# Two key tiles weighed in one go, and whole-array jobs moved to the other gaps, in a 1444-key cross attention

## What is computed

```python
qm = _split_heads(q @ Wq.T + bq)
km = _split_heads(k @ Wk.T + bk)
vm = _split_heads(v @ Wv.T + bv)
scores = jnp.einsum('bnlh,bnph->bnlp', qm, km) / np.sqrt(HEAD_DIM)
scores = jnp.where(mask, scores, MASK_FILL)
attn = jax.nn.softmax(scores, axis=-1)
out = jnp.einsum('bnlp,bnph->bnlh', attn, vm)
out = out.transpose(0, 2, 1, 3).reshape(B, L, D_MODEL)
return out @ Wo.T + bo
```

## Time and profile before

| | |
|---|---|
| median of the runs | 2277.2 us |
| span of the profiled execution | 2267.4 us |
| stage B, from its first weighing to the end of the full clock | 602 to 1736 us |
| one group of four elements in stage B | 144.4 us, 36.1 per element |
| PE, DVE, ACT busy in stage B | 93%, 78%, 64% |
| granted TensorE clock in stage B | 1.00 |

### The profile page before, as it was taken

One profiled execution on the slowest core, in us unless ns is written; L12 is line 12 of the kernel. 1 busy time (PEld: TensorE's weight loads), 2 busy tenths in 40 slices (PEclk: granted clock), 3 DMA queues, 4 the chain that ended last, 5 costly groups with the idle time before them and its releaser, 6 DMA issues. The chain is left out here.

```text
span 2267.4 us, 43146 instructions
## 1 busy us (share of the span) xinstructions
PE 1969.0 (87%) x16922; PEld 1258.0 (55%) x16922; DVE 1578.2 (70%) x3726; ACT 1324.7 (58%) x2169; POOL 551.4 (24%) x477
## 2 busy tenths in 40 slices
PE   3679999667999999999999999999997888888997
PEld 2546666444556556565565655556564555555554
DVE  4845666795787877878788788878771566664554
ACT  3645776683366666666666666666664555553444
POOL 1411322314122212222221222222222132311122
PEclk9879999777799999999999999999998788788999
DMA  5025554012132323233131322313222001103441
GB/s 153 1 92 183 184 173 142 4 37 91 65 109 74 126 68 118 78 105 119 68 126 63 120 85 101 121 66 122 79 89 67 16 8 16 31 1 59 67 71 40
DMA packets 120023, 189.26 MB, mean 83 GB/s; under 512 B 36770, under 2 KB 94090, under 8 KB 118414
## 3 DMA queue, kind: packets, MB, share of 16 engines
q1 hardware_dynamic: 119822, 186.50, 26.6%
HBM read 103.33 MB, written 11.76 MB: 51 GB/s over the span
## 5 line engine op out<-in xcount | busy, mean ns | idle before, releaser
L1610 DVE TENSOR_REDUCE b_part_max<-psum 128x1 f32<-128x482 f32 (+3 forms) x1248 | 737.6, 651 | 188.1 <-PE psum L1487 174.1
L1400 ACT ACTIVATE b_PT<-psum 128x800 f32<-128x800 f32 x768 | 616.6, 836 | 386.1 <-PE psum L1506 381.1
L1487 PE MATMUL psum<-b_KH,b_QBD 64*128 64x482 f32 (+1 forms) x1152 | 422.6, 445 | 45.7 <-DVE b_part_max L1610 43.3
L1506 PE MATMUL psum<-b_QS,b_KS 64*128 64x200 f32 x3072 | 438.3, 288 | 0.5 <-ACT b_PT L1400 0.3
L1506 PEld LDWEIGHTS psum<-b_QS,b_KS 64*128 64x128 f32 x3072 | 339.4, 186 | 16.2 <-issue 11.8
L1522 PE MATMUL psum<-b_PT,b_V 128*32 128x200 f32 x6144 | 341.4, 339 | 0.6 <-ACT b_PT L1400 0.6
L1487 PEld LDWEIGHTS psum<-b_KH,b_QBD 64*128 64x128 f32 x1152 | 197.3, 189 | 198.6 <-DVE b_part_max L1610 118.4
L1322 POOL TENSOR_TENSOR b_KL<-b_KF,b_KH 128x1444 fp32r<-128x1444 f32 x32 | 106.8, 3338 | 693.3 <-PE psum L1506 670.1
L1522 PEld LDWEIGHTS psum<-b_PT,b_V 128*32 128x32 f32 x6144 | 159.9, 109 | 149.1 <-ACT b_PT L1400 82.3
L1900 ACT ACTIVATE c_HE<-psum,C 128x400 f32<-128x400 f32 x128 | 75.7, 595 | 94.6 <-PE psum L2116 90.1
L1474 PE MATMUL psum<-W,b_CT 128*128 128x128 f32 (+1 forms) x768 | 117.7, 293 | 12.6 <-DVE b_part_max L1610 6.7
(11 more groups left out here) (280 smaller groups left out, 3095.2 us busy)
## 6 DMA issues: line engine op xcount, KB each, us to landing
b_KS<-b_KH SPq DMA_DIRECT2D x64, 722.0 KB
a_CT<-in_ctxt SPq DMA_DIRECT2D x32, 722.0 KB, 5.5
b_CT<-in_ctxt SPq DMA_DIRECT2D x32, 722.0 KB, 4.4
b_KS<-b_KL SPq DMA_DIRECT2D x32, 722.0 KB
a_CN<-in_ctxn SPq DMA_DIRECT2D x32, 704.0 KB
att_scratch<-b_AO SPq DMA_DIRECT2D x32, 200.0 KB, 1.9
c_G<-gates_scratch SPq DMA_DIRECT2D x4, 1600.0 KB
c_KBD<-gates_scratch SPq DMA_DIRECT2D x4, 1600.0 KB
```

Source lines behind the costliest of these rows:

```text
L1400: nc.scalar.activation(PT[:, kt % 2, 2 * a:2 * a + 2, :], psum[:, 2 * a:2 * a + 2, 0:TG], ACT.Exp).then_inc(sem["pt_ready"], 1)
L1487: m = mm(bank(b, D, size), QBD[rows, j % 2, tile * D:(tile + 1) * D], KH[rows, j % 2, at_:at_ + size], start=True, stop=True)
L1506: m = mm(bank(p, D, 2 * T, (s % 2) * 2 * T), KS[rows, j % 2, s, kt * D:(kt + 1) * D], QS[rows, j % 2, s * 2 * T:(s + 1) * 2 * T], start=Tr ...
L1610: v.tensor_reduce(part_max[0:rows, q, c:c + 1], bank(b, rows, CHUNKS[c][1]), AX.X, ALU.max)\
```

## The change

Two key tiles are weighed one after the other after each odd slot, none after an even one. All whole-array jobs get the even slots: values 0, 2, 4 (before 2, 3, 4), left-over maxima 0, 4, 6 (before 5, 6, 7), keys 6, 8, 10 (before 6, 7, 8), the result 2 (before 1), the turn 8 as before, queries 0 and 10 (before 0 and 5). `PT` gets a third buffer. Four maximum jobs stand in slots 9, 10, 11, 0, 1 and 6, three in 2 to 5, none in 7 and 8; before it was four in 9, 10, 11 and 0, three in 1 to 6, two in 7, none in 8. In ACT's program a key chunk whose job is in slot s is now rounded after the exponentials of tile s + 1, as value chunks are copied.

```diff
-MAIN_TILES = ((9, 2, 2), (10, 2, 2), (11, 2, 2), (0, 2, 2), (1, 2, 1), (2, 1, 2), (3, 2, 1), (4, 1, 2), (5, 2, 1), (6, 1, 2), (7, 1, 1))
-QUERY_SLOTS = (((0, 0), (1, 0), (2, 0), (3, 5)), ((4, 0), (5, 5)), ((6, 0),), ())
+MAIN_TILES = ((9, 2, 2), (10, 2, 2), (11, 2, 2), (0, 2, 2), (1, 2, 2), (2, 1, 2), (3, 2, 1), (4, 1, 2), (5, 2, 1), (6, 2, 2))
+QUERY_SLOTS = (((0, 0), (1, 0), (2, 0), (3, 10)), ((4, 0), (5, 10)), ((6, 0),), ())
+VALUE_SLOTS, LEFT_SLOTS, KEY_SLOTS = (0, 2, 4), (0, 4, 6), (6, 8, 10)
+RESULT_SLOT, TURN_SLOT = 2, 8
...
-        PT = sb("PT", [D, 2, HG, TG])
+        PT = sb("PT", [D, 3, HG, TG])
...
                 if a == 0:
-                    wait(act, sem["pv_done"], n * KT + (kt - 1))
+                    wait(act, sem["pv_done"], n * KT + (kt - 2))
...
-                        if kt - 3 in range(len(highs)):
-                            value(*place(g, j, highs[kt - 3]), g, j + 1, kt - 3)
-                        if kt - 8 in range(len(keys)):
-                            high_keys(*place(g, j, keys[kt - 8]), g, j + 2, kt - 8)
+                        for i, at in enumerate(highs):
+                            if kt == VALUE_SLOTS[i] + 1:
+                                value(*place(g, j, at), g, j + 1, i)
+                        for i, at in enumerate(keys):
+                            if kt == KEY_SLOTS[i] + 1:
+                                high_keys(*place(g, j, at), g, j + 2, i)
...
                         some(PHASES * kt + 4)
-                        weigh(g, j, kt)
+                        if kt % 2:
+                            weigh(g, j, kt - 1)
+                            weigh(g, j, kt)
```

More of the change, by code:

```diff
@@ L1100, in ring_jobs @@
     after = not last or j + 2 < GROUP
-    jobs = [((g, j + 1, "result", 0), PHASES * 1 + 4)]
+    jobs = [((g, j + 1, "result", 0), PHASES * RESULT_SLOT + 4)]
     for i, (_, _, _, kt, p) in enumerate(MAINS):
@@ L1109, in ring_jobs @@
     if nxt:
-        jobs += [((g, j + 1, "value", r), PHASES * (r + 2) + 4) for r in range(3)]
-        jobs += [((g, j + 1, "max", len(MAINS) + c), PHASES * (c + 5) + 4) for c in range(3)]
-        jobs.append(((g, j + 1, "turn", 0), PHASES * 8 + 4))
+        jobs += [((g, j + 1, "value", r), PHASES * VALUE_SLOTS[r] + 4) for r in range(3)]
+        jobs += [((g, j + 1, "max", len(MAINS) + c), PHASES * LEFT_SLOTS[c] + 4) for c in range(3)]
+        jobs.append(((g, j + 1, "turn", 0), PHASES * TURN_SLOT + 4))
     if after:
-        jobs += [((g, j + 2, "key", r), PHASES * (r + 6) + 4) for r in range(3)]
+        jobs += [((g, j + 2, "key", r), PHASES * KEY_SLOTS[r] + 4) for r in range(3)]
     return sorted(jobs, key=lambda job: job[1])
@@ L1398, in exponent @@
                 if a == 0:
-                    wait(act, sem["pv_done"], n * KT + (kt - 1))
-                nc.scalar.activation(PT[:, kt % 2, 2 * a:2 * a + 2, :], psum[:, 2 * a:2 * a + 2, 0:TG],
+                    wait(act, sem["pv_done"], n * KT + (kt - 2))
+                nc.scalar.activation(PT[:, kt % 3, 2 * a:2 * a + 2, :], psum[:, 2 * a:2 * a + 2, 0:TG],
                                      ACT.Exp).then_inc(sem["pt_ready"], 1)
@@ L1522, in weigh @@
                         m = mm(psum[32 * r:32 * r + 32, 6, b * 2 * T:(b + 1) * 2 * T], V[:, j % 2, kt, 4 * b + r, :],
-                               PT[:, kt % 2, 2 * b + r // 2, (r % 2) * 2 * T:(r % 2 + 1) * 2 * T],
+                               PT[:, kt % 3, 2 * b + r // 2, (r % 2) * 2 * T:(r % 2 + 1) * 2 * T],
                                start=(kt == 0 and b == 0), stop=(kt == KT - 1), tile_position=(0, 32 * r),
```

## The result

The changed kernel takes 2325.4 us in the median against 2279.5 for the kernel before, measured side by side: 1.0213 times the time before, with an interval of 1.0182 to 1.0244.

The account below looks back on a forecast made before the run. PE and DVE, neither saturated, were taken as bound through a ring of three banks; slot lengths gave 149.67 us a group against 144.41, eight groups 42 us, so 2277.2 becomes 2319 us, range 2298 to 2342.

Parts of the forecast that it names:

- The mechanism: Stage B: without weighing between, maxima follow whole-array jobs whose banks are unread; during pairs DVE runs dry; 5.26 us more a group.
- The pair of weighings: After odd slots on PE: the second weighing takes 0.68 instead of 0.82, a pair 1.50, saving 0.84 us per element.
- The third maxima: Slots 9, 11 and 1: the third maximum waits for a bank, until 0.88 in slot 9 and 1.83 in slot 11.
- the sum: Stage B's slot lengths added up: four elements take 149.67 us against 144.41, 5.26 more; eight groups make 42 us.
- Slots 7 and 8: No maxima, bound by ACT, whose key rounding stands ahead of tile 8's exponentials: 2.31 and 2.38 us.
- Slot 4: Even slot with a value chunk and a left-over job: 1.23 + 1.09 + 0.22 = 2.54 us.
- the last element: End of stage B: the last group was counted the same as the others, 5.26 us more.
- the ring: Three banks between PE's maxima and DVE's reductions in stage B; they bind both engines, and neither is saturated.
- The saved passages reach the end: Rival: only PE's work counts, so 1.4 us x 32 = 45 us are gained, 2232; faster of any size 9 in 100.
- Both sides meet: Rival: losses in slots 8 to 1 are three tenths smaller, 4.57 to 3.2, nothing is left: 2277; 6 in 100.
- The clock falls too: Rival: the clock falls in slots 7 and 8 of each element, 53 us more, 2372; 5 in 100.
- DVE's idle ahead of the reductions: Sign in the changed profile: this idle time should grow from 23.5 us a group, since DVE's work is the same.

Follow-up runs that it names:

- the late rounding: The changed kernel with the first two key chunks rounded one slot later on ACT: 1.0187 times the time before, a group of 147.4 us.
- neither edit: The changed kernel with one half only: weighing in pairs with the tables of before, 1.0199 times the time before; new tables with single weighings, 1.0054.
- the pair alone: The changed kernel with the job tables of the kernel before, so only weighing in pairs and PT's third buffer remain: 1.0199 times the time before.
- the fastest kernel: The changed kernel with three maxima in every slot, single weighings and whole-array jobs clumped in slots 2, 4, 7 and 8: 2156.1 us, 0.9456.

## Why the prediction came out right

**The mechanism and the sizes of its steps.** The pair of weighings took 1.50, as taken. The third maxima waited 0.89, 1.83 and 1.46, where the sum had 0.88, 1.83 and 1.46 (slot 1: left-over job read at 1.41, and the start right behind it). The slots of the element, start to start, against the sum: slot 9 3.36 (3.40), slot 10 with the query 3.48 (3.48), slot 11 4.30 (4.35), slot 0 3.78 (3.78), slot 1 3.93 (3.98), slot 2 3.00 (2.99), slot 3 3.02 (3.0), slot 5 2.93 (3.0), slot 6 3.36 (3.38), slot 7 2.34 (2.31), slot 8 2.37 (2.38). So slots 8 to 1 take 21.22 us for the 16.80 of before, 4.42 lost (4.57 in the sum), and slots 2 to 7 take 17.47 for 20.42, 2.95 gained (3.20). The group comes out at 150.2 against 149.67. Slots 7 and 8, bound by ACT behind the early rounding, were foreseen in size, but the prediction counted them as a gain (4.69 for the 5.52 of before) and did not say that with the late rounding they would take 3.99. That this and not the banks is the half of the loss that neither edit makes alone was not foreseen, and the experiments' own first theory had it wrong.

**One slot was mis-sized.** Slot 4 took 2.80 where the sum had 2.54: the value chunk begins 1.24 into it as supposed (1.23), lasts 1.20 up to the left-over job behind it, not 1.09, and this lasts 0.36 up to the next slot's first maximum, not 0.22. The three rows:

```profile
1252.94 1.27 PE L1478 MATMUL psum<-W,b_CT 128*128 128x128 f32 x8
1254.14 0.43 PE L1488 MATMUL psum<-b_KH,b_QBL 128*64 128x482 f32 x1
1254.50 0.48 PE L1491 MATMUL psum<-b_KH,b_QBD 64*128 64x480 f32 x1
```

**The step that failed is the last element.** The sum counted its group like the other seven, 5.3 us more. It was 14.5 more: 5.5 in the first three elements, and 9.0 in the last. In that element there are no maxima, so the ring plays no part; scores, exponentials and weighings are all that is left. PE's timeline in it, two slots at full clock:

```profile
1765.48 0.70 PE L1510 MATMUL psum<-b_QS,b_KS 64*128 64x200 f32 x8
1767.10 1.42 PE L1510 MATMUL psum<-b_QS,b_KS 64*128 64x200 f32 x8 [0.91 <-ACT b_PT L1402]
1768.45 1.57 PE L1526 MATMUL psum<-b_PT,b_V 128*32 128x200 f32 x32
1769.94 0.70 PE L1510 MATMUL psum<-b_QS,b_KS 64*128 64x200 f32 x8
```

A pair of slots takes 4.46 (1765.48 to 1769.94). PE waits 0.91 for an exponential, then weighs 1.5 us, in which ACT runs out of scores. It is the ring's story over again with ACT in DVE's place. Before, two slots took 3.79 here:

```profile
1713.80 1.42 PE L1506 MATMUL psum<-b_QS,b_KS 64*128 64x200 f32 x8
...
1717.59 1.41 PE L1506 MATMUL psum<-b_QS,b_KS 64*128 64x200 f32 x8
```

Between the first and the last of its twelve blocks of scores lie five and a half pairs of slots; at 0.67 more each that is an estimated 3.7 of the 9.0. The other 5.3 go with the clock, which falls three times in this element, at 1752.6, 1773.1 and 1779.9. Windows at the first two falls:

```profile
1750.00:1752.60 2.60, 2.13 (x28) 1.71 (x32) 0.00 (x0) 2.49 (x4) 0.00 (x0) 1.00 0.21 41
1752.60:1756.00 3.40, 2.49 (x28) 1.48 (x17) 0.00 (x0) 1.63 (x4) 0.00 (x0) 0.50 0.19 34
...
1773.00:1776.00 3.00, 3.00 (x36) 1.74 (x36) 0.00 (x0) 0.85 (x2) 0.00 (x0) 0.51 0.00 0
```

With the last group's 14.5 in place of 5.3 the forecast's 42 us for stage B would have been 51, and the time 2328. The profile has 54.7 us in stage B; the runs have 46 by the medians and 49 by the ratio. So the sum was short by 13 us of what the profile shows. That the forecast nevertheless lies only 6 us below the median (2.3 of them because the kernel before took 2279.5 beside it and not 2277.2) is in part luck. The two profiled executions lie further apart than the medians do, and why the stretch behind stage B was 10.4 us longer in one of them stays open.

**The rivals.** *The saved passages reach the end*: its condition was slot 9 without the wait of 0.88 and slots 11 and 1 in 3.2; the trace has 0.89, 4.30 and 3.93. PE was spared its passages and lost them to DVE. *Both sides meet*: slots 8 to 1 came to 21.2 us (21.37 in the sum), where this rival needed 20.0. *The clock falls too* named slots 7 and 8 of each element, where it stayed up; it fell in the last element of the changed kernel, in six places of the pair alone ahead of its last element, and in two of the late rounding, so it was right in kind and wrong in place.

**Wrong in "what would show it".** DVE's idle ahead of the reductions was to grow from 23.5 us. It did not. By line, over one group:

```profile
L1616 DVE TENSOR_REDUCE b_part_max<-psum 128x1 f32<-128x482 f32 (+2 forms) x157 | 92.5, 649 | 21.5 <-PE psum L1491 17.8 <-PE psum L1488 3.5
...
L1624 DVE CAST b_NMH<-psum 13x128 fp32r<-13x128 f32 x4 | 1.1, 279 | 12.3 <-PE psum L1495 12.3
```

The idle went in front of the turn's copy, which is the first thing DVE does after slots 7 and 8 without maxima; before it was 3.4 us there:

```profile
L1618 DVE CAST b_NMH<-psum 13x128 fp32r<-13x128 f32 x4 | 1.1, 278 | 3.4 <-PE psum L1491 3.4
```

Idle time is put down to the instruction that ends it, so two empty slots show up under whatever happens to come next.

## What to carry to other kernels

When two engines are tied by a short ring of buffers, the work that doesn't touch the ring is what lets the other engine catch up: keep one such piece between every two bursts, and make no burst longer than the ring. Merging those pieces saves a passage of 0.14 us each and cost 2 to 12 us a group here; even bursts and few interrupted slots gave 5.4% of the whole time. Where an engine works in a fixed order, look also at what stands behind its waits: a copy of 0.59 us moved one place ahead cost 2.9 us a group, but only in slots that had nothing else to do meanwhile. And count the last round of a loop for itself: an element that lacks one of the streams has another bound.

## What was not expected of the hardware

PE's busy time is no measure of its work here: the same matmuls were 133.9 us busy in a group of before and 126.9 in the fastest kernel. PE's granted clock, at the upper level of 2.4 GHz through all regular groups of before and after, went to the lower one in kernels that differ only in the order of their work: after stretches such as 1.76 us busy of 4, behind a DMA wait, after 2.13 of 2.60, and, in the groups of the pair alone, after stretches in which PE's waits were 0.31 at most. What decides it these profiles don't tell. And an order can bring work ahead of its loads: the waits of up to 3.2 us at a DMA came with a load that was issued 2.5 us later, counted from the group's first score, than in the kernel before, for a job that kept its slot.
